# Layer 1 attention: P summed over four key tiles before the products with ones, with the new additions half on VectorE and half on GpSimd

## The reference, cut to what matters

```python
dots = jnp.einsum('bhid,bhjd->bhij', q, k) * scale      # b = 4, h = 8 heads of dh = 32, n = 3136
attn = jax.nn.softmax(dots, axis=-1)
out = jnp.einsum('bhij,bhjd->bhid', attn, v)
out = out.transpose(0, 2, 1, 3).reshape(b, n, d)
return out @ w_out + b_out
```

## Time and profile before

| | |
|---|---|
| median of three runs | 9473.03 us |
| profiled execution | 9507.64 us, its span 9505.8 us |
| TensorE busy | 8490.4 us, 89% of the span |
| VectorE busy | 5516.6 us, 58% |
| ScalarE busy | 4254.8 us, 45% |
| GpSimd busy | 3424.1 us, 36% |
| layer 1 attention | from 2927.4 to 7826.1 us of the span |

### The profile page before, as it was taken

The page is one execution under the profiler, slowest core; times in us unless marked ns, Lnnn a source line. Parts: engine busy times, 40 slices in busy tenths (PEclk is TensorE's granted clock), DMA queues, the critical chain, the costliest instruction groups (busy, mean ns, idle before and its releaser), DMA issues. The chain is left out here.

```text
span 9505.8 us, 154680 instructions
## 1 busy us (share of the span) xinstructions
PE 8490.4 (89%) x47120; PEld 4664.0 (49%) x47120; DVE 5516.6 (58%) x13138; ACT 4254.8 (45%) x9220; POOL 3424.1 (36%) x2082
## 2 busy tenths in 40 slices
PE   4499998999898999999999999999999887178888
PEld 3255554555565555554554545555454336145555
DVE  3355555555567977676776767777675005134444
ACT  1155555555320055655555555555556661011111
POOL 3000000000120066666666666666666662421221
PEclk8655555555796599999999999999999998589999
DMA  5411112110484011212112121111212006121110
GB/s 147 91 17 13 22 22 38 22 22 8 127 256 112 3 27 33 58 26 62 33 28 55 33 51 33 43 38 33 58 26 51 4 17 180 33 64 28 47 42 15
DMA packets 439310, 480.37 MB, mean 51 GB/s; under 512 B 163096, under 2 KB 401290, under 8 KB 434151
## 3 DMA queue, kind: packets, MB, share of 16 engines
q1 hardware_dynamic: 415015, 426.26, 18.6%
q0 software_dynamic: 23424, 43.45, 1.7%
HBM read 298.78 MB, written 180.34 MB: 50 GB/s over the span
## 5 line engine op out<-in xcount | busy, mean ns | idle before, releaser
L1177 DVE TENSOR_REDUCE a_tops<-a_ps 128x1 f32<-128x448 f32 (+1 forms) x5600 | 3071.0, 612 | 1079.7 <-PE a_ps L1079 1062.5
L1277 ACT ACTIVATE a_P<-a_ps 128x448 f32<-128x448 f32 (+1 forms) x5600 | 2656.4, 547 | 2110.8 <-PE a_ps L1148 2078.8
L1300 POOL TENSOR_TENSOR a_added<-a_P 128x896 f32<-128x896 f32 x1344 | 2799.5, 2102 | 2081.5 <-ACT a_P L1277 2081.5
L1148 PE MATMUL a_ps<-a_qp,a_kp 98*128 98x448 f32 (+1 forms) x5600 | 2152.4, 399 | 96.8 <-ACT a_P L1277 72.5
L1079 PE MATMUL a_ps<-a_hk,a_hq 96*128 96x448 f32 (+1 forms) x4900 | 1818.0, 381 | 1.3 <-DMA a_hq<-scratch_q 1.3
L1148 PEld LDWEIGHTS a_ps<-a_qp,a_kp 98*128 98x128 f32 (+1 forms) x5600 | 1028.7, 187 | 1286.0 <-ACT a_P L1277 735.1
L1099 PE MATMUL a_ps<-a_P,a_vt 128*32 128x448 f32 (+1 forms) x11200 | 1332.6, 548 | 0.0
L459 DVE CUSTOM_DVE_ANT_0 n_sm<-n_ps,n_bias 112x448 f32<-112x448 f32 x928 | 577.9, 624 | 851.4 <-PE n_ps L390 851.4
L1079 PEld LDWEIGHTS a_ps<-a_hk,a_hq 96*128 96x128 f32 (+1 forms) x4900 | 916.0, 187 | 262.8 <-DVE a_tops L1177 170.0
L485 ACT ACTIVATE n_P<-n_sm,n_mx 112x448 f32<-112x448 f32 x928 | 619.7, 668 | 846.3 <-DVE n_mx L459 846.3
L400 PE MATMUL n_ps<-n_idn,n_P 112*112 112x112 f32 x3712 | 923.4, 404 | 21.5 <-DVE n_P L466 21.5
(11 more groups left out here) (177 smaller groups left out, 6397.5 us busy)
## 6 DMA issues: line engine op xcount, KB each, us to landing
a_qp<-scratch_q SPq DMA_DIRECT2D x168, 224.0 KB, 3.8
a_kp<-scratch_k SPq DMA_DIRECT2D x96, 320.0 KB, 5.1
a_hk<-scratch_k SPq DMA_DIRECT2D x84, 336.0 KB, 5.2
scratch_t<-o_ts SPq DMA_DIRECT2D x56, 448.0 KB, 5.1
a_hq<-scratch_q SPq DMA_DIRECT2D x84, 200.0 KB, 3.1
e_w<-in_w SPq DMA_DIRECT2D x16, 1024.0 KB
a_hq<-scratch_q SPq DMA_DIRECT2D x84, 192.0 KB, 3.5
p_xs<-in_x SPq DMA_DIRECT2D x4, 3136.0 KB, 15.5
```

Source lines behind the costliest of these rows:

```text
L1148: pe.matmul(PS[0:rows_of(t), i_s % 3, 0:GW], kp[0:98, hh, 128 * t:128 * t + rows_of(t)], qp[0:98, hh, GW * j:GW * j + GW], start=True, sto ...
L1177: dve.tensor_reduce(tops[0:rows_of(t), KT * hh + t, k:k + 1], PS[0:rows_of(t), bank, 0:GW], AX_X, ALU.max).then_inc(topped, 1)
L1277: act.activation(P[0:rows_of(t), (2 * n + pair) % (2 * RING), hh % 2, :], PS[0:rows_of(t), (4 * n + hh) % 3, 0:GW], ACT.Exp).then_inc(expe ...
L1300: pool.tensor_tensor(added2[:, a % 6, :, :], P[:, (2 * n + pair) % (2 * RING), :, :], P[:, (2 * n + 2 + pair) % (2 * RING), :, :], ALU.add ...
```

## The change

TensorE now takes the products with ones once per four steps: six times per group instead of twelve (`sum_four`), in the burst of step 4v + 3 + 6. GpSimd still adds P of two steps, and the two pair-sums of four steps (four tiles: two halves by two pairs) are then added up: pair 0 on VectorE, in place, at the start of the step 4v + 3 + 2 and before the step's maxima (`four` on VectorE), pair 1 on GpSimd, right after its four additions (`four` on GpSimd). The last tile of a group (`t` = 24) is multiplied with ones directly, as before. Two semaphores are new, `four_left` and `four_right`. To have room for them, the semaphores of layer 0's attention are cleared and freed at the end of that stage, with a barrier of all engines behind it.

```diff
@@ layer0_attend
-            return ctx.enter_context(nc.semaphore("n0_" + name))
+            sems.append(nc.alloc_semaphore("n0_" + name))
+            return sems[-1]
+        sems = []
...
+    nc.clear_and_free_semaphores(sems)
+    nc.all_engine_barrier()
@@ layer1_attend
-        SUMS = PAIRS + 1
+        FOURS = KT // 4
+        SUMS = FOURS + 1
+        QF = FOURS * NG
-        SUM_LAG = 3
+        SUM_LAG, FOUR_LAG = 6, 2
...
-                if t % 2 == 1:
-                    sums.append((n, (n // STEPS, j, t // 2)))
+                if t % 4 == 3:
+                    sums.append((n, (n // STEPS, j, t // 4)))
...
+        def sum_slot(f, pair):
+            return 2 * (f % 2) + pair
+        def part_slot(f, pair):
+            return 4 + pair
@@ tensor
-            def sum_pair(q, j, u):
-                pe.wait_ge(added, q * (2 * PAIRS * NG) + 2 * (PAIRS * j + u) + 2)
-                if u == 0:
+            def sum_four(q, j, v):
+                pe.wait_ge(four_left, q * QF + FOURS * j + v + 1)
+                pe.wait_ge(four_right, q * QF + FOURS * j + v + 1)
+                if v == 0:
                     since(pe, sums_taken, q, NG, j)
                 for hh in range(4):
                     last = pe.matmul(PS[HD * hh:HD * hh + HD, SUM, 0:GW], ones[:, :],
-                                     added2[:, (2 * (PAIRS * j + u) + hh // 2) % 6, hh % 2, :],
-                                     start=(u == 0), stop=SUM_NUMBER[j, u] == LAST_SUM[j])
+                                     added2[:, sum_slot(FOURS * j + v, hh // 2), hh % 2, :],
+                                     start=(v == 0), stop=SUM_NUMBER[j, v] == LAST_SUM[j])
                 last.then_inc(summed, 1)
@@ vector
+            def four(q, f):
+                dve.wait_ge(added, q * (2 * PAIRS * NG) + 2 * (2 * f + 1) + 1)
+                dve.tensor_tensor(added2[:, sum_slot(f, 0), :, :], added2[:, sum_slot(f, 0), :, :],
+                                  added2[:, part_slot(f, 0), :, :], ALU.add).then_inc(four_left, 1)
+            FOUR_AT = [KT * (f // FOURS) + 4 * (f % FOURS) + 3 + FOUR_LAG for f in range(QF)]
...
                 for n in range(STEPS):
+                    if n in FOUR_AT:
+                        four(q, FOUR_AT.index(n))
+                    if n + STEPS in FOUR_AT and not first:
+                        four(q - 1, FOUR_AT.index(n + STEPS))
                     while more and i < maxima_by(n + 1):
@@ gpsimd
+            def add_steps(q, f, half, pair):
+                n = KT * (f // FOURS) + 4 * (f % FOURS) + 2 * half
+                if half == 0:
+                    if pair == 0:
+                        before, at = divmod(f - 2, QF)
+                        since(pool, summed, q + before, SUMS * NG, SUM_NUMBER[at // FOURS, at % FOURS])
+                    slot = sum_slot(f, pair)
+                else:
+                    since(pool, four_left if pair == 0 else four_right, q, QF, f)
+                    slot = part_slot(f, pair)
+                pool.wait_ge(exped, q * HS + 4 * (n + 1) + 2 * pair + 2)
+                pool.tensor_tensor(added2[:, slot, :, :], P[:, (2 * n + pair) % (2 * RING), :, :],
+                                   P[:, (2 * n + 2 + pair) % (2 * RING), :, :], ALU.add).then_inc(added, 1)
+            def four(q, f, pair):
+                pool.wait_ge(added, q * (2 * PAIRS * NG) + 2 * (2 * f + 1) + pair + 1)
+                pool.tensor_tensor(added2[:, sum_slot(f, pair), :, :], added2[:, sum_slot(f, pair), :, :],
+                                   added2[:, part_slot(f, pair), :, :], ALU.add).then_inc(four_right, 1)
             def quad(q):
-                ...
+                for f in range(QF):
+                    for half in range(2):
+                        for pair in range(2):
+                            add_steps(q, f, half, pair)
+                    four(q, f, 1)
```

More of the change, by code:

```diff
@@ L837, in layer1_attend @@
         inverted, divided = sem("inverted"), sem("divided")
+        four_left, four_right = sem("four_left"), sem("four_right")
         stored = [sem("stored0"), sem("stored1")]
@@ L878, in bursts @@
                 mixes.append((n // STEPS, n % STEPS))
-                if t % 2 == 1:
-                    sums.append((n, (n // STEPS, j, t // 2)))
+                if t % 4 == 3:
+                    sums.append((n, (n // STEPS, j, t // 4)))
                 parts = []
[L882 to L886, removed]
+                while sums and sums[0][0] <= n - SUM_LAG:
+                    parts.append(("sum",) + sums.pop(0)[1])
+                while mixes and mixes[0][0] * STEPS + mixes[0][1] < n:
+                    parts.append(("mix",) + mixes.pop(0))
                 out.append(parts)
@@ L899, in layer1_attend @@
                 elif part[2] % KT == KT - 1:
-                    order.append((part[1], part[2] // KT, PAIRS))
+                    order.append((part[1], part[2] // KT, FOURS))
         own = [(j, u) for quad, j, u in order if quad == 0]
@@ L1105, in mix @@
                                          P[0:rows, (2 * n + hh // 2) % (2 * RING), hh % 2, :], start=False,
[L1106 removed]
+                                         stop=SUM_NUMBER[j, FOURS] == LAST_SUM[j])
                     last.then_inc(summed, 1)
[L1109 to L1112 removed]
+            def sum_four(q, j, v):
+                pe.wait_ge(four_left, q * QF + FOURS * j + v + 1)
+                pe.wait_ge(four_right, q * QF + FOURS * j + v + 1)
+                if v == 0:
                     since(pe, sums_taken, q, NG, j)
@@ L1124, in burst @@
                     else:
-                        sum_pair(q + part[1], part[2], part[3])
+                        sum_four(q + part[1], part[2], part[3])
             def quad(q, first, more):
@@ L1225, in quad @@
                 if not more:
+                    for f in range(QF):
+                        if FOUR_AT[f] >= STEPS:
+                            four(q, f)
                     for part in range(4):
@@ L1272, in quad @@
                                 if t0 == KT - 1:
-                                    act.wait_ge(summed, (q + before) * (SUMS * NG) + SUM_NUMBER[j0, PAIRS])
+                                    act.wait_ge(summed, (q + before) * (SUMS * NG) + SUM_NUMBER[j0, FOURS])
                             if t0 < KT - 1:
@@ L1289, in _ @@
         def _(pool):
+            def add_steps(q, f, half, pair):
[15 more added lines that the diff above has]
+                                   added2[:, part_slot(f, pair), :, :], ALU.add).then_inc(four_right, 1)
             def quad(q):
-                for j in range(NG):
-                    for u in range(PAIRS):
+                for f in range(QF):
+                    for half in range(2):
                         for pair in range(2):
[L1294 to L1301, removed]
+                            add_steps(q, f, half, pair)
+                    four(q, f, 1)
             pool.memset(kp[96:98, :, :].bitcast(F32), 1.0).then_inc(cleared, 1)
```

## The result

The changed kernel takes 9735.92 us (median of four runs, 9724.58 to 9757.82) against 9477.10 us for the kernel before (9468.98 to 9484.09, four runs): a ratio of 1.0276, 95% interval 1.0253 to 1.0299. It is slower by 259 us. The forecast said slower by 143 us: the sign and the range held, the size was too small.

What follows compares the result with a forecast made beforehand. TensorE's own stream was taken as the bound. Gains of 231 us (220 - 10 + 21) against losses of 374 us (346 + 12 + 14 + 2) made it 143 us slower: 9616 us from the median, range 9380 to 9800.

Steps and rivals of the forecast that it cites:

- Who comes first: VectorE's addition against GpSimd's fifth: cost depends on whether VectorE arrives before the fifth starts; otherwise it is blocked.
- Products with ones: TensorE, first seven quads: halving them gains 220 us, of which 10 us are lost at quads' ends.
- The last quad: No maxima there, TensorE's steps shrink: 3 us gained per group, 21 us in all (0 to 31).
- VectorE's additions, 346 us: Delay to TensorE from VectorE's new additions: 49 us per quad, 346 us over seven quads.
- four and four products, comes first: Neither step has five maxima products: VectorE first by 0.07 us, 0.3 us lost, 16 per quad.
- five in the second step, blocked: VectorE arrives 0.47 us after GpSimd and is blocked: 1.9 us lost, 10 per quad.
- five in the first step, blocked: VectorE 0.16 us behind GpSimd: three in four blocked at 2.1 us, the rest 0.2; 11 per quad.
- four and four products, t = 9, blocked: An inversion of 0.83 us in front makes VectorE late: blocked at 2.3 us, three per quad.
- rival 1: VectorE nearly always first, as GpSimd's fifth addition may start late: 112 us losses against 231, 9354 us; chance 0.19.
- rival 2: GpSimd always first, so VectorE's additions are blocked: 202 us more, 9818 us; chance 0.14.
- rival 3: The 11 additions 0.16 us behind GpSimd are not blocked, but for two: 88 us less, 9528 us; chance 0.17.
- rival 4: Shifted engines let most additions fall into GpSimd's pauses; gain and loss cancel, 9473 us; chance 0.08.

Runs made afterwards that it cites:

- first: Changed kernel with VectorE's two-input addition replaced by a one-input reduction, result thrown away, so the sums are incomplete: 9394.1 us, 0.9919 of the kernel before.
- third: Changed kernel, complete, with GpSimd's fifth addition also waiting for VectorE's addition of the same four steps: 9414.08 us, 0.9941 of the kernel before.
- sixth: Changed kernel, complete, with TensorE's burst before the last maxima products in six steps per group: 9460.42 us, 0.9949 of the kernel before.
- fourth experiment: Changed kernel, complete, with both new additions on GpSimd and none on VectorE: 9752.48 us, 1.0297 of the kernel before.
- experiment 28: Not a run: in "fourth experiment 28 of 56 divisions" the 28 counts divisions, in the changed kernel with both additions on GpSimd, 9752.48 us.
- second experiment: Changed kernel without VectorE's addition, only its semaphore counted up, so the sums are incomplete: 9289.01 us, 0.9807 of the kernel before.
- both: Changed kernel, complete, with GpSimd's fifth addition waiting for VectorE's and TensorE's burst moved early: 9394.5 us, 0.9877 of the kernel before.
- ninth kernel: Changed kernel, complete, with VectorE's addition behind the first maximum of its step instead of in front: 9617.5 us, 1.0106 of the kernel before.

## Why the prediction was right, and where it was not

**The mechanism was right.** A two-input VectorE instruction stands still behind a GpSimd addition, the maxima behind it are late, and TensorE waits before its burst. The first, third and sixth experiments each take one link away (the second input, the order of arrival, what is queued on TensorE) and each brings back over 3%.

One reading under "Who comes first" was too wide. It took from a cast that a waiting VectorE instruction gets in between two GpSimd additions that stand back to back; in the fourth experiment 28 of 56 divisions did not get in at the next such place. In the changed kernel the forecast held all the same, because the fifth addition waits for the fourth to be complete: a pause of 0.08 us each time, and 85 of the 113 short additions begin while the fourth still runs.

**Gains.** Products with ones: the page has 348.0 us for 2688 of them, before 648.3 for 5376, though at the lower clock some take longer; where no addition disturbs, the seven quads gain 162 us, forecast 184. In the 1196 steps that neither the kernel before nor the second experiment spent at the lower level the gain is 183.6 us; the other 29 steps, next to the quads' ends, lose 21 us of it, at least in part by the clock: 106 us at the lower level against 48. The last quad gained some 30 us, forecast 21. There VectorE's addition holds GpSimd by 0.73 us, not 0.97:

```profile
7799.27 2.84 POOL L1339 TENSOR_TENSOR a_added<-a_added 128x896 f32<-128x896 f32 x1
7802.07 8.27 POOL L1333 TENSOR_TENSOR a_added<-a_P 128x896 f32<-128x896 f32 x4
7810.42 2.84 POOL L1339 TENSOR_TENSOR a_added<-a_added 128x896 f32<-128x896 f32 x1
```

Five additions take 7810.42 - 7799.27 = 11.15 us, so 6 x 11.15 = 66.9 us per group; without VectorE's addition the quad takes the same 469.0 us, 67.0 per group. So it is not VectorE's hold on GpSimd that sets this time; TensorE is taken to be the bound, with GpSimd just as full (465.40 of the 470 us in the window above).

**The term that was mis-sized: VectorE's additions, 346 us.** Measured 454 us. The classes were right. Behind steps with four and four products the additions take 1.15 us on average (105 in the first seven quads, forecast first by 0.07 us), but 2.32 us at t = 9 (21); with five in the second step 2.46 us (56), with five in the first 2.54 us (63, 49 of them blocked, three in four as taken). The 21 steps at t = 9 are the longest, 7.2 us on average. What was missing is the clock. The same step at t = 9 in another quad:

```profile
4743.78 0.74 PE L1094 MATMUL a_ps<-a_hk,a_hq 96*128 96x448 f32 x1 [2.31 <-DVE a_tops L1193]
...
4745.20 1.72 PE L1131 MATMUL a_ps<-a_added,a_ones 128*32 128x448 f32 x8
4746.69 1.15 PE L1114 MATMUL a_ps<-a_P,a_vt 128*32 128x448 f32 x8
```

The wait is the same 2.31 us, but then eight products take 1.72 us instead of the 0.96 of before, and the step 7.81 us instead of 6.37; the window around it (4735 to 4751) has a clock of 0.89.

Two comparisons with the kernel without VectorE's addition (second experiment) separate the clock from the waits, over the seven quads. By sums: TensorE stands idle 278 us more (331.8 against 53.3) and is busy 176 us longer (3949.2 against 3773.6) with the same products. It spends 286 us more at the lower level (392 against 106), and half of that, 143 us, is the most that the lower level can have cost. By steps: in steps that neither kernel spent at the lower level, a step with an addition is longer than the same step without it by

| | forecast, us | measured, us (steps) |
|---|---|---|
| four and four products, comes first | 0.3 | 0.31 (90) |
| five in the second step, blocked | 1.9 | 1.71 (30) |
| five in the first step, blocked | 2.1 | 1.86 (30) |
| four and four products, t = 9, blocked | 2.3 | 2.32 (5) |

With such prices for all steps the additions cost some 310 us. This is an estimate, and a low one if the longer waits are those that lower the clock. The remaining 140 us or so lie in the 163 of 1225 steps in which one of the two kernels was at the lower level, and fit under the 143. So the waits were forecast a little too high (346 us), and the clock, at some 140 us, was the missing term. No kernel here held the waits and kept the clock, so the split stays an estimate. The time at the lower level went with the waits in the other kernels: 101 us at the lower level with the waiting fifth addition, 133 with the early burst, 113 with both, 299 in the ninth kernel, where 138 us of waiting were left, and 518 in the fourth, where TensorE was idle for 354 us.

The Trainium skill ("TensorE: Matmul & The Clock Gate", HAM oscillation — how this bites in real kernels) describes that waits between groups of products can let the clock fall again and again, each fall paid anew. The trace agrees with that pattern: 75 stretches where there were 6, with waits for the maxima of at most 2.5 us.

**The additions that come first are not free.** Forecast 84 us if none is blocked; the third kernel, where nearly none is, takes 3944.3 us for the seven quads, 117 us over the second kernel. The difference lies at t = 9: there the inversion stands in front, and an addition that comes first still costs 0.98 us (49 steps), elsewhere 0.31 us. This, and 22 us less of gain, is why rival 1 (9354 us) came to 9414 when the third experiment made it true.

**Smaller terms.** The division: 0.90 us on average in the first seven quads against 0.6 alone, 14 us as taken, though not on the path each time. The barrier: no difference measured. GpSimd's pauses and the slots of P: hidden, as forecast; GpSimd's idle time before its first additions is still 1464.7 us.

**The rivals.** Rival 1 fails on the count: 113 of 294 additions are short, not nearly all; rival 2 on the same number; rival 3 on the 2.54 us; rival 4 on the sign. The point that the forecast left open, where the fifth addition's start lies, came out between: 21 of the 117 VectorE additions that start up to 0.4 us after the start shown for GpSimd's fifth still come first (5373.92 against 5373.56 above), of the 62 that start later, while the fifth runs, none does.

## What to carry to other kernels

Before giving VectorE a two-input instruction beside a busy GpSimd, ask who will be first each time, and settle it by a semaphore where the engine that waits has time: that line was worth 3.3% here. A delay costs what is queued behind it: put the work that needs nothing (the burst) in front of the product that waits. And leave pauses in GpSimd's row, for without them two-input work on VectorE may not come to its turn.

## What the runs showed that was not expected

- A GpSimd row without pauses can keep VectorE out across instructions: the division took over 10 us in 28 of 56 cases, up to 71.4 us (in the last quad), and 1.10 us in the median, at most 2.54, once each addition waited for the one before (pauses of 0.17 us). The Trainium skill ("SBUF — State Buffer", Who interferes with whom) says, of VectorE's two-port modes, that whoever issues first gets the shared ports for its whole instruction and the other is fully blocked. Here, with two inputs in SBUF, the block reached over up to 34 further additions, and the measurement decides.
- It works both ways: GpSimd's fifth addition takes 2.10 us alone and 2.82 to 3.39 us where VectorE is in.
- Waits of TensorE of at most 2.5 us (215, 1.6 us in the median), spread over steps that are otherwise full, brought 392 us at the lower clock where there had been 48.
- A VectorE addition of 128 x 896 with two inputs takes as long alone as a reduction with one (1.07 us each).
